# Feed-forward set-up steps placed inside the attention: 4-bit weight tables, the first codes and the first 512 rows

## The reference, cut to what matters

```python
x = x + _layernorm(_L0_attn_ref(_layernorm(x), Wqkv, Wo))          # 2 x 1024 tokens of 512, 32 heads of 16, one key/value head, ALiBi, causal
x = x + _layernorm(_L0_ffn_ref(_layernorm(x), ...4-bit weights))   # silu(x@Wg) * (x@Wu) @ Wd, inner width 1376
x = x + _layernorm(_L1_attn_ref(_layernorm(x), ...))               # a block-masked linear layer
x = x + _layernorm(_L1_ffn_ref(_layernorm(x), ...))                # a linear layer with a Fourier update
# 4-bit weights: W[k,n] = scales[g_idx[k],n] * (w4[k,n] - (z4[g_idx[k],n] + 1)), eight codes packed in an int32
```

## Time and profile before

| | us |
|---|---|
| median of three runs | 1397.24 (1396.83 to 1401.67) |
| the profiled execution, its own time | 1395.92 |
| its span in the trace | 1394.1 |
| last attention store issued, from the span's start | 747.83 |
| first instructions of `ffn` | 753.37 |
| first product of the feed-forward | 799.73 |

### The profile page before, as it was taken

How to read it: one execution, slowest core, us unless ns; L and a number is a source line. 1 busy time by engine, 2 the same in 40 slices (tenths; PEclk the granted TensorE clock), 3 DMA queues, 4 the chain that set the end, 5 groups by cost and what they waited for, 6 DMA issues and landing times. The chain is left out here.

```text
span 1394.1 us, 16630 instructions
## 1 busy us (share of the span) xinstructions
PE 1239.7 (89%) x6208; PEld 826.8 (59%) x6208; DVE 730.3 (52%) x1353; ACT 571.8 (41%) x1006; POOL 308.0 (22%) x329
## 2 busy tenths in 40 slices
PE   4599999999999999989992389999999999579995
PEld 4567456555554656544541257778778788346664
DVE  4376785786688887723214666342141210365553
ACT  5143455265456565556661344311111111034443
POOL 0121141111110101011124344411121111115554
PEclk9999999899999999999996599999999999889998
DMA  6534223201221012122001422230020010130303
GB/s 194 112 54 113 43 40 106 40 2 39 47 56 25 23 19 40 25 40 40 18 31 51 124 72 62 94 106 0 0 91 1 0 61 1 59 105 1 121 0 120
DMA packets 60942, 75.97 MB, mean 54 GB/s; under 512 B 14738, under 2 KB 37530, under 8 KB 60796
## 3 DMA queue, kind: packets, MB, share of 16 engines
q1 hardware_dynamic: 57252, 64.42, 18.7%
q0 software_dynamic: 2560, 8.39, 1.7%
q10 hardware_dynamic: 1056, 2.16, 0.4%
HBM read 53.46 MB, written 21.59 MB: 54 GB/s over the span
## 5 line engine op out<-in xcount | busy, mean ns | idle before, releaser
L792 DVE TENSOR_REDUCE mx<-bank 128x1 f32<-128x512 f32 (+2 forms) x576 | 367.3, 685 | 138.7 <-PE bank L910 85.1
L734 ACT ACTIVATE PT<-ST 128x512 f32<-128x512 f32 x576 | 313.3, 600 | 210.3 <-PE ST L975 90.0
L907 PE MATMUL bank<-KS,QS 126*128 126x512 f32 (+2 forms) x896 | 253.3, 365 | 18.1 <-DMA QS<-pos_scratch 15.8
L975 PE MATMUL ST<-QS,KS 128*128 128x512 f32 x576 | 240.1, 457 | 5.0 <-DMA QS<-mparts 4.1
L907 PEld LDWEIGHTS bank<-KS,QS 126*128 126x128 f32 x896 | 158.7, 197 | 82.9 <-DVE mx L792 37.7
L975 PEld LDWEIGHTS ST<-QS,KS 128*128 128x128 f32 x576 | 108.3, 195 | 82.6 <-ACT PT L734 64.1
L989 PE MATMUL PO<-PT,V 128*32 128x512 f32 x1152 | 152.2, 604 | 1.6 <-ACT PT L734 1.6
L51 PE MATMUL f_pair<-f_xT,gu 128*128 128x512 f32 (+1 forms) x352 | 142.1, 404 | 0.0
L1495 DVE TENSOR_TENSOR f_h<-f_h,f_pair 128x512 f32<-128x512 f32 (+1 forms) x44 | 30.2, 686 | 210.1 <-ACT f_h L1402 210.1
L53 PE MATMUL f_pair<-f_xT,gu 128*128 128x512 f32 (+1 forms) x352 | 139.8, 397 | 0.0
L52 PE MATMUL f_pair<-f_xT,gu 128*128 128x512 f32 (+1 forms) x352 | 139.4, 396 | 0.0
(11 more groups left out here) (181 smaller groups left out, 1777.6 us busy)
## 6 DMA issues: line engine op xcount, KB each, us to landing
QS<-q_scratch SPq DMA_DIRECT2D x48, 256.0 KB
q_scratch<-QP SPq DMA_DIRECT2D x24, 256.0 KB, 2.3
l_x<-x_dram SPq DMA_DIRECT2D x12, 512.0 KB, 4.2
xres<-_attn_hidden_states_dram POOLq DMA_DIRECT2D x16, 256.0 KB, 3.0
x_dram<-xout POOLq DMA_DIRECT2D x16, 256.0 KB, 2.4
f_xin<-x_dram SPq DMA_DIRECT2D x4, 1024.0 KB, 7.0
f_xsum<-x_dram SPq DMA_DIRECT2D x4, 1024.0 KB, 6.9
x_dram<-f_xsum SPq DMA_DIRECT2D x4, 1024.0 KB, 4.8
```

Of the source, the lines that this page charges most:

```text
L734: act.activation(PT[:, quad % PT_RING, n % 4, :], ST[:, n % ST_RING, :], ACT.Exp).then_inc(p_done, 1)
L792: v.tensor_reduce(mx[:, i % 2, z, h:h + m], at(u).rearrange("p (m k) -> p m k", m=m), AX.X, ALU.max).then_inc(bank_free_dve, 1)
L907: last = pe.matmul(at(u)[:, j * w:(j + 1) * w], hi(QS[0:ROWS1, slot, h + j, :]), hi(KS[b][0:ROWS1, k0:k0 + w]), start=(j == 0 or not diag) ...
L975: last = pe.matmul(dst, hi(KS[b][0:ROWS2, kb * P:(kb + 1) * P]), hi(QS[0:ROWS2, slot, h:h + 4, :]), start=True, stop=not diag)
```

## The change

What `ffn` did ahead of its early pieces now stands in `attention`:

- `PIECES` has a sixth entry, `AFTER`: the first 512 rows of the attention's own output. SP loads them from HBM into `xin`, DVE normalizes them, and PE, ACT and DVE turn and split them into `xT`, which is now the same memory as the feed-forward's `f_xT0`. `xin` is one buffer for both parts too.
- The tables are made in steps called "clear" and "fetch" (POOL), "index", "onehot", "zeros", "scales" (DVE), "part" (ACT) and "dt" (19 small matmuls on PE in five groups, each with a bank of the ring, copied by ACT). The two first units of codes are loaded by SP and unpacked by DVE there as well ("codes").
- The planner orders these steps with costs of its own. They become ready when the maxima of query block 10 begin (`AFTER_AT`), and rank behind other work that could start at the same time. The planner's cost of "norm" on DVE goes from 1700 to 2300 ns, which also holds for piece 1 at the start.
- The loads of group indices, scales and zero points are now issued by POOL, 18 DMAs in a row; before, 6 of them were issued by SP at the end of `attention` and 12 by SP in `ffn`.
- Buffers: the codes and the one-hot table lie where the attention's `wx0` and `wx1` were, the zero-point table and unpacked codes where `QP` was, so "clear" waits for the last projection (`("kv", NC - 1)`) and the last query store.
- In `ffn`, SP starts with the load of block 1's rows and then the third unit of codes; PE starts with the six early pieces and goes on to block 0's products without transposes between; DVE starts with the scaling of the first piece. `load_codes` and `unpack_codes` are the old functions, moved out of `ffn`.

The core of the diff:

```diff
...
+TABLE_STEPS = ("index", "onehot", "zeros", "scales", "codes", "dt", "part")
+AFTER_AT = 10
...
+AFTER = NC
+PIECES.append((0, 0, 4))
...
-    took = {"p1": 232, "tile": 232, "pv": 1060, "xt": 400, "q": 700, "kv": 700, "vt": 400, "mt": 200, "ot": 400, "at": 400, "wo": 700}
+    took = {"dt": 400, "p1": 232, "tile": 232, "pv": 1060, "xt": 400, "q": 700, "kv": 700, "vt": 400, "mt": 200, "ot": 400, "at": 400, "wo": 700}
...
+        elif j[0] == "codes":
+            free["sp"] = t + 2400
+            end["codes", j[1]] = t + 6000
...
-            for i, k in ((1, 2), (4, 3), (6, 4)):
+            for i, k in ((1, 2), (4, 3), (6, 4), (AFTER_AT, AFTER)):
                 if u == maxima_of(i)[-1]:
                     open_piece(k)
+            if u == maxima_of(AFTER_AT)[0]:
+                sp_issue(("load", AFTER), e)
+                pend["pool"].append((("clear",), e))
+                for k in range(CODE_RING):
+                    sp_issue(("codes", k), e)
...
-                out.append((max(t, free[e]), 1 if j[0] in ("exp", "stats") else 0, k, j))
+                out.append((max(t, free[e]), 1 if j[0] in ("exp", "stats") + TABLE_STEPS else 0, k, j))
...
-            f = t + {"mx": 200, "mt": 280, "ot": 700, "stats": 900, "ys": 1150, "vt": 300, "kv": 750, "norm": 1700}.get(kind, 690)
+            f = t + {"mx": 200, "mt": 280, "ot": 700, "stats": 900, "ys": 1150, "vt": 300, "kv": 750, "norm": 2300, "index": 900, "onehot": 1200,
+                     "zeros": 2700, "scales": 1650, "codes": 2600}.get(kind, 690)
...
-                add_piece(j[1], [t + 560 * (x + 1) + reads["dve"] for x in range(3)])
+                add_piece(j[1], [t + 560 * (x + 1) + reads["dve"] for x in range(4)])
...
-            f = t + {"rstd": 1000, "norm": 8400, "fin": 5300}[kind]
+            f = t + {"rstd": 1000, "norm": 8400, "fin": 5300, "clear": 5000, "fetch": 14000}[kind]
...
+                if k == AFTER:
+                    src = x1_dram
+                    for i in range(2):
+                        sp.wait_ge(x1_out[i], 16 * 2)
+                sp.dma_start(xin[:, t % 4:t % 4 + n, :], src[rows, :].rearrange("(t p) d -> p t d", p=P)).then_inc(x_in[k % 2], 16)
...
-            for dst, src in next_loads:
-                sp.dma_start(dst, src, allow_slow_non_contiguous=True).then_inc(next_in, 16)
-            sp.wait_ge(next_in, 16 * len(next_loads))
...
+                elif kind == "codes":
+                    if i == 0:
+                        full(sp, ("kv", NC - 1))
+                    load_codes(sp, mats, dq, i)
...
+            def clear_tables():
+                full(pool, ("kv", NC - 1))
+                pool.wait_ge(q_out, 128 * NC)
+                pool.memset(dq.zpacked, 0).then_inc(cleared, 1)
+                pool.memset(dq.s_raw, 0.0).then_inc(cleared, 1)
+                pool.memset(dq.tables, 0.0).then_inc(cleared, 1)
+                pool.memset(dq.ztab, 0.0).then_inc(cleared, 1)
+
+            def fetch_tables():
+                for dst, src in table_loads:
+                    pool.dma_start(dst, src, allow_slow_non_contiguous=True).then_inc(ids_in, 16)
+                pool.wait_ge(cleared, 4)
+                for m in range(3):
+                    g0, g, w = FIRST_GROUP[m], GROUPS_OF[m], D if m == 2 else INTER
+                    for i in range(3):
+                        pool.dma_start(dq.s_raw[i * G_ROWS + g0:i * G_ROWS + g0 + g, 0:w], mats[m][1]).then_inc(s_in, 16)
+                    pool.dma_start(dq.zpacked[g0:g0 + g, 0:w // PACK], mats[m][2]).then_inc(z_in, 16)
...
+                elif kind == "dt":
+                    n = min(4, DQ_COLS - u[1])
+                    act.wait_ge(cleared, 4)
+                    act.activation(dq.onehotT[0:S_ROWS, u[1]:u[1] + n, :], at(u)[0:S_ROWS, 0:n * P].rearrange("p (u k) -> p u k", k=P),
+                                   ACT.Copy).then_inc(bank_free_act, 1)
...
+            def scale_part(k):
+                if k == 0:
+                    act.wait_ge(s_in, 16 * 9)
+                else:
+                    act.wait_ge(s_rest, 1)
+                act.activation(dq.s_part, dq.s_raw, ACT.Copy).then_inc(s_part_done, 1)
...
+                elif kind == "dt":
+                    pe.wait_ge(onehot_done, 1)
+                    for k in range(min(4, DQ_COLS - u[1])):
+                        last = pe.matmul(dst[0:S_ROWS, k * P:(k + 1) * P], dq.onehot[:, u[1] + k, :], identb[:, :], start=True, stop=True)
...
-    uses = [("dq", 0, j) for j in EARLY_PIECES] + [("xt", 0, t) for t in range(4)]
+    uses = [("dq", 0, j) for j in EARLY_PIECES]
...
-            sp.dma_start(xin[:, :, :], rows(x1_dram, 0)).then_inc(x_in, 16)
-            sp.wait_ge(cleared, 2)
-            for m in range(3):
-                g0, g, w = FIRST_GROUP[m], GROUPS_OF[m], D if m == 2 else INTER
-                sp.dma_start(zpacked[g0:g0 + g, 0:w // PACK], mats[m][2]).then_inc(z_in, 16)
-                for i in range(3):
-                    sp.dma_start(s_raw[i * G_ROWS + g0:i * G_ROWS + g0 + g, 0:w], mats[m][1]).then_inc(s_in, 16)
-            sp.wait_ge(tables_done, 2)
-            for u in range(len(UNITS)):
-                load_codes(u)
-                if u == 2 * CODE_RING + 2:
-                    sp.wait_ge(turned, 4)
-                    sp.dma_start(xin[:, :, :], rows(x1_dram, 1)).then_inc(x_in, 16)
+            sp.dma_start(xin[:, :, :], rows(x1_dram, 1)).then_inc(x_in, 16)
+            for u in range(CODE_RING, len(UNITS)):
+                load_codes(sp, mats, dq, u)
             sp.wait_ge(picked, len(DQ))
-            sp.wait_ge(q4_done, len(UNITS))
...
-            pool.memset(zpacked, 0).then_inc(cleared, 1)
-            pool.memset(s_raw, 0.0).then_inc(cleared, 1)
-            pool.memset(tables, 0.0).then_inc(blank, 1)
-            pool.memset(ztab[:, :], 0.0).then_inc(blank, 1)
...
-            block_rstd(0)
...
-            for u in range(CODE_RING):
-                codes(u)
-            row_moments(0)
-            normalize(0)
...
-            for t in range(4):
-                xt_lo(0, t)
...
-            pe.wait_ge(onehot_done, 1)
-            for a in range(DQ_COLS):
-                if a == 16:
-                    pe.wait_ge(onehotT_done, 1)
-                pe.matmul(turn[:, a // 4 % 4, a % 4 * P:(a % 4 + 1) * P], onehot[:, a, :], identb[:, :], start=True, stop=True).then_inc(onehot_turned, 1)
-            pe.wait_ge(onehotT_done, -(-DQ_COLS // 4))
-            pe.wait_ge(tables_done, 2)
...
-            for t in range(4):
-                transposes(0, t)
...
+            dq = Unpack(
+                gidx=gidx, group_ids=group_ids, shifts=shifts,
+                qw=early[:, 0:CODE_RING * 1024].bitcast(I32).rearrange("p (s n) -> p s n", s=CODE_RING),
+                q4=xsum[:, 0:CODE_RING, :].bitcast(BF16),
...
+                ztab=xsum[:, 2:4, :].bitcast(BF16).rearrange("p t n -> p (t n)")[:, 0:INTER],
+                s_raw=s_raw[0:S_ROWS, :],
+                onehot=onehot[:, :, :],
...
```

390 lines of the change are left out of this document (220 added, 170 removed).

## The result

The changed kernel takes **1356.82 us** (median of four runs, 1351.60 to 1357.31). The kernel before took 1397.75 beside it (four runs, 1396.83 to 1401.67). The ratio is 0.9694, with a 95% interval of [0.9663, 0.9724]. The gain is 41 us by the medians and 43 by the ratio, where 31.8 were forecast. The profiled execution took 1356.86, its span is 1355.1, and the difference of the two spans is 39.0 us. It is on the small side, since the profiled execution of the kernel before (1395.92) was one of its faster ones.

A forecast was written before the change was run, and what follows sets the result against it. The prediction took PE as the bound (busy 89% of the span), idle at the feed-forward's start. -29.5 + 3.0 - 3.3 - 2.0 = -31.8 us, so a median of about 1365.4, range 1355 to 1379.

The forecast's parts named there:

- lead of the feed-forward: Start of the feed-forward: first product at 770.2 instead of 799.7 us, since only the six early pieces stay; -29.5 us.
- PE's added work: Attention: 19 small matmuls and 16 transposes on PE, 3.0 of their 3.5 us counted as path; low end 0.
- late order of the attention: Late attention: PE's 3.29 us wait at 624.51 for query block 14's slot goes; -3.3 us.
- start of the attention: Start of the attention: PE's 9.94 us wait before 70.33 for block 1's slot is partly filled; -2 us (-6 to 0).
- border between the parts: Between last attention store and first feed-forward instruction: 0 in the table, with no term of its own in the forecast's sum.
- behind block 0's store: Rest of the feed-forward and `layer1`: same order as before, 0 us.
- DVE priced at 0: Attention: about 21 us of new DVE work against 11 free, absorbed by PE's order; 0, far end +10 us.
- The rival at 1375: Attention: it pays for DVE's added steps, with only four banks; +10 us, 1375; chance 0.17 for 1372 to 1380.
- The reordering gives more: Rival: full 6 us at the start, PE's added work vanishes, codes land early; -43 us, 1354; chance 0.11 for below 1358.
- POOL's loads: Attention: POOL's issues end by 490; rival: slow index loads hold ACT, then PE, about 1426; chance 0.04.
- Memsets beside reductions: Attention: POOL's four memsets beside DVE's reductions from PSUM cost nothing; +6.1 us if they blocked those too.

The follow-up runs named there:

- Kernel 4: Changed kernel with the feed-forward's load of block 1's rows issued behind the fifth unit's codes, not ahead of the third's; 1352.99 us.
- kernel 3: Kernel before, its own attention steps in the order of the changed kernel's planner, none of the new work; 1380.22 us.
- kernel 7: Changed kernel with the one-hot comparison done nine times, not once, 10 us more DVE work in a row; 1366.45 us.
- kernel 2: Changed kernel with the planner's "norm" cost put back to 1700 ns for the old normalizings, 2300 kept for the new piece; 1361.68 us.
- kernel 5: Changed kernel with ten more memsets of the tables (35 us) on POOL ahead of its scale loads; 1376.49 us.
- kernel 1: Kernel before with only the planner's cost of "norm" on DVE changed, 1700 to 2300 ns; 1393.17 us.
- Kernel 9: Kernel 4 with eight more, unused semaphores in the attention; 1351.51 us (one run).
- kernel 6: Changed kernel with only tables and first codes made in the attention, block 0's rows handled in the feed-forward as before; 1363.67 us.
- kernel 10: Kernel 4 with four early pieces, the two of the first down projection put behind the first gate product; 1358.60 us.
- kernel 11: The changed kernel itself, run and profiled a second time; 1354.59 us.

## Why the prediction was right and wrong

Term by term, in us of the span. Start, late order and added work are means over the profiles, as worked out above and below; the rest is from the two profiles of the result.

| term | forecast | measured |
|---|---|---|
| lead of the feed-forward | -29.5 | -29.9 |
| PE's added work | +3.0 | +2.5 |
| late order of the attention | -3.3 | -6.2 |
| start of the attention | -2.0 | -5.9 |
| border between the parts | 0 | +1.5 |
| behind block 0's store | 0 | -2.2 |
| sum | -31.8 | -40.2 |

The start (3.9 us short) and the late order (2.9 short) are the misses. The two terms at 0 went opposite ways.

**The lead of the feed-forward: right, slightly low.** Forecast: first product at +16.8 us, gain 29.5. Measured: +14.94, 31.4 at the first product and 29.9 at block 0's store, which is the part of it that lasts. Two pieces were scaled 4.1 us after the start (749.92 + 0.69), as worked out, and DVE then waited once for the third unit of codes. It landed at +8.2 us, not +9.6: I had charged half a megabyte at the full 1 MB load's pace behind it. The chain from there to the product took 6.8 us against 7.2. Kernel 4 shows that the 1 MB load ahead of the codes is the cause of that wait.

**PE's added work: right.** 3.0 forecast, 2.5 measured (kernel 3 against the profiles with the work).

**DVE priced at 0: right, for too good a reason.** From the turn of block 9 to that of block 15 PE waited only once for more than a quarter of a microsecond in the changed kernel, and that was for a slot of `QS`, not for a reduction:

```profile
654.71 1.29 PE L1157 MATMUL bank<-KS,QS 126*128 126x128 f32 x8 [1.94 <-DMA QS<-pos_scratch]
```

But there was no slack for 10 us in one piece: kernel 7 pays 9.6 for them. The rival at 1375 had the right mechanism, and the change as the planner spread it stayed under the point where it begins.

**The start of the attention: the term that was mis-sized.** "So I count -2 (from -6 to 0)", since DVE might set the pace behind the filled wait. The wait at 70.33 became this one:

```profile
68.53 0.50 PE L1157 MATMUL bank<-KS,QS 126*128 126x256 f32 x2 [3.22 <-DMA QS<-pos_scratch]
```

At block 9's turn the twelve profiles with the new start stand at 477.3 us in the mean (474.8 to 480.2), the two with the old one (before and kernel 2) at 483.2. The gain is 5.9 us, my far end; the first profile had only 3.4 of it. DVE did not take it back. Waits that I hadn't looked at changed too. PE's 1.43 us at 268.15 went, and the clock, granted at 0.90 from 250 to 300 us, is at 0.97 or 1.00 now. A wait of 2.90 us at 38.84 for DVE's `xT` is filled with block 0's maxima, and what is left is 0.37 us at 36.39. Two of 2.29 and 1.14 us at 194.87 and 196.89 are new. How the 5.9 us are made up of these, no run takes apart, so that the sum came to my far end is partly chance.

**The late attention: the step that failed.** I took 3.3 us for one wait (624.51) and held the rest of the order for neutral. The wait did go. But kernel 3 gives 6.2 us for the order alone: the three longer waits together shrank from 6.39 to 2.73 us, the short ones by 0.6, and 2.1 lie inside PE's busy time, at a mean clock of 0.99 in both. What these 2.1 us are stays open. I had looked at one wait and not at what all of PE's waits behind block 9, and the time inside its busy stretches, amount to. "The reordering gives more" was a rival at 1354, and its time was met, but only one of its three terms: the start gave 5.9 of its 6 us, while PE's added work was paid (2.5 of 3 us) and the product came 1.9 us earlier than forecast and not 4. What was missing from its sum came from the late order, which it had left at 3.3, so that its time was met is luck.

**POOL's loads: right.** Memsets and loads on POOL, first the largest memset, then the first and the last load issue:

```profile
469.28 3.53 POOL L830 MEMSET early<- 128x4096 bf16 x1
...
473.93 0.78 POOL L835 DMA_DIRECT2D gidx<-in_L_ffn_gate_g_idx_dram  x1
...
483.56 0.51 POOL L841 DMA_DIRECT2D f_h<-n_L_ffn_down_qzeros_dram  x1
```

They end at 484.1 (forecast: by 490), and ACT's scale copy at 498.92 waits for nothing. The slack was 13.7 us (kernel 5), 11 were estimated. The rival took 30 ns an element for the index loads, 72 us in all, and this the DMA issues of the profile could have settled beforehand. The largest index load (5.0 KB, so 1280 elements), with its time from issue to landing in us at the end, issued by SP in the kernel before, then by POOL now:

```profile
gidx<-in_L_ffn_down_g_idx_dram SPq DMA_DIRECT2D x1, 5.0 KB, 2.5
```

```profile
gidx<-in_L_ffn_down_g_idx_dram POOLq DMA_DIRECT2D x1, 5.0 KB, 3.6
```

That is under 3 ns an element. Of the rule on strided last dimensions (the Trainium skill, DMA: Bandwidth & Descriptors, "Rules for kernel authors") the trace shows the price at these sizes, not the count of descriptors: 0.76 to 0.78 us to issue an index load against 0.51 for one of rows, and the 3.6 us to land. Nothing waited for these loads.

**Memsets beside reductions: right.** While POOL's memset of 3.53 us ran, DVE's reductions kept their time:

```profile
470.68 1.89 DVE L988 TENSOR_REDUCE mx<-bank 128x2 f32<-128x512 f32 x3 [0.67 <-PE bank L1157]
...
472.87 0.69 DVE L988 TENSOR_REDUCE mx<-bank 128x4 f32<-128x512 f32 x1 [0.30 <-PE bank L1160]
```

The index CAST, 5.91 us beside memsets, takes 0.18 with POOL at rest:

```profile
500.97 0.18 DVE L1061 CAST d_gf<-gidx 128x18 f32<-128x18 int32 x1
```

This agrees with the rule of the Trainium skill (SBUF — State Buffer, "SBUF: two separate sides"). The page limits the case of two SBUF inputs to a GpSimd instruction that reads SBUF, which the prediction left out; a memset reads nothing, so here this changes nothing.

**Not in the sum.** The border became 1.5 us longer, in all eleven profiles with the new attention work and in none of the three without (before, 1 and 3). Kernel 9 rules one cause out; the real one is open. Behind block 0's store 2.2 us went. 0.7 of them are in the feed-forward's later blocks, and the kernels with the changed feed-forward all have them (kernel 6, with the old steps at its start, a third); why is open. 1.6 are in `layer1`, whose code is the same and which took 179.5 before and 177.9 after. It took 177.2 us in kernel 3, 178.4 in kernel 1 and 180.5 in kernel 6, so I take this for scatter between profiles; that isn't shown.

## What to carry over

When a list scheduler orders the work, an added step changes everything behind it: price the new order as a term of its own, by summing all waits of the bound engine in the stretch, and measure it by running the new order without the new work, because a part of it (2.1 of 6.2 us here) shows in no wait. An engine with a fifth of its time free can still be full at a place, so test the room by adding work, not by the busy share. And an earlier first product is no gain by itself: look at the next mark at which the engines meet again (kernel 10 won 6 us at the one and lost 3.7 at the other).

## What the runs showed of the hardware that was not expected

The same program with the same order came to block 9 at 480.2 us in one profile and at 476.3 in another. Some 1.1 us of it was there at the first block; from the turn of block 5's maxima to that of block 8 it took 177.0 us in the first, 175.5 in three other kernels of this order and 173.9 to 174.0 in the eight others. The steps of 1.5 us go with ten microseconds at a granted clock of 0.83, as in the rows under kernel 11. PE's bracketed waits alone don't decide it: around the start of these ten microseconds both profiles of the changed kernel have the same two, 0.31 and 0.33 us, and only the first has the dip. In the kernel before, waits of 1.10 and 1.43 us (260.01 and 268.15) stand beside ten microseconds at 0.62. What sets the clock in such a stretch is open.

POOL waits for DVE too, not only DVE for POOL. POOL's `pow` on one column, 0.56 us at 462.33, took 1.92 beside a DVE step with two SBUF inputs, and ended 0.43 us after it. POOL's timeline, then DVE's:

```profile
519.03 1.92 POOL L809 TENSOR_TENSOR yrstd<-ymom,half_neg 128x1 f32<-128x1 f32 x1 [34.95 <-DVE ymom L1053]
```

```profile
518.87 1.65 DVE L1097 SCALAR_TENSOR_TENSOR early<-f_h,group_ids,d_s_raw 54x1376 bf16<-54x1376 bf16 x1
```
